# A transformer block on one core: three 1 MB transfers per sequence move from SyncE's queue to ScalarE's

## The chip, the cores and the metric

One core of a Trainium2 chip runs the whole program. The metric is device time in microseconds (us), launch to end.

## The reference, cut to what matters

Sixteen sequences x of 512 tokens by 512 features, float32, go through one attention layer of 32 heads of 16 and one gated feed-forward layer:

```python
q, k, v = split_heads(layernorm(x) @ Wq.T + bq), ...          # 16 sequences, 32 heads of 16
q, k = apply_rope(q, freqs), apply_rope(k, freqs)
weights = softmax(where(causal, q @ k.T / 4, -inf))
x1 = x + layernorm((weights @ v) @ Wo.T + bo)
g, u = layernorm(x1) @ gate_w.T * gate_s, layernorm(x1) @ up_w.T * up_s
out = x1 + layernorm((silu(g) * u) @ down_w.T * down_s)
```

## The kernel before, in words

The program has two phases one after the other: attention (`attention_phase`), which writes x1 to memory, and the feed-forward layer (`ffn_phase`), which reads it. The change touches attention alone.

Each engine runs a list written out by hand. `body(i)`, a pass, has 40 steps: 8 groups of 5 (step s = 5g + u). In each step TensorE makes a piece of the raw scores (`mx`, L864), whose row maxima VectorE takes (L753), and a piece of the transposed scores (`ts`, L878), which ScalarE exponentiates into `probs` (L587, 40 per pass). GpSimd masks `probs` (L465), TensorE weighs the values with them (L892). `ts` has one buffer, so TensorE cannot write the scores of step s+1 before ScalarE has read those of step s. Since there are just 40 exponentials in a pass, their starts mark the steps: below, "group 5 of a pass" is the stretch from its exponential 25 to its exponential 30.

The projections ride in the same steps. Queries and keys are projected for the next pass, get their bias on ScalarE (`biased`, L572), are rotated by GpSimd (`turned`, `roped`, L444 to L453) and VectorE (L735), split into `half` by ScalarE (L581) and VectorE (L740), and go through memory to be laid out anew: SyncE sends `half` to `slots` (L316, L317, at u = 1) and fetches them as `qT` or `kT` (L327, at u = 3), which waits for the sending. The weighed values `oT` (L598) go to memory as `weighed` (L342, at u = 4); their row sums are fetched (`sums`, L349), inverted, sent (`recips`, L355) and fetched again spread over the rows (`spread`, L363) with the values (`averaged`, L364). GpSimd multiplies the two (L484, "the average" below) in groups 1, 3, 5 and 7, at u = 1, ahead of the rotation of its group; ScalarE (L547) and VectorE (L728) split the product.

All transfers stand in SyncE's list (the SP queue), in a fixed order by step. Three of them carry 1 MB, once per pass:

- `xn<-x` at step 9 (L393): the sequence of pass i+2, for its statistics on VectorE at steps 15 and 16 (L705). It waits until `xn` has been transposed (`xT_full`).
- `x<-xr` at step 14 (L396): x1 of sequence i-2 to memory. It waits for GpSimd's residual sums (L491, steps 6 and 11; `x1_ready`).
- `xr<-x` at step 19 (L399): the sequence i-1 for its residual. It waits for the one before (`x1_out`).

There are 15 passes with a `xn` load and 15 with an `xr` load besides the two first loads, which stay where they are (L291, L298), and 16 with an x1 store: 46 transfers. `body` runs from pass -1 to pass 17. A pass before 0 or after 15 has no exponentials.

ScalarE also normalises x (L559, steps 19 to 21) and the projected output (L565, steps 5, 6, 9, 10).

Of the kernel before, what the change touches and what calls it, by code (L numbers as in the profile page):

```python
# [31 lines left out]
NT = T // P  # L32
NC = C // P
# [37 lines left out]
def attention_phase(nc, x, wT, bias_row, bias_columns, rope_cos, rope_sin, slots, weighed, recips, x1):  # L71

    ctx = ExitStack()
    with ctx:
        def sb(name, shape, dt=F32):
            return ctx.enter_context(nc.sbuf_tensor(name, shape, dt))
# [4 lines left out]
        def sem(name):  # L81
            return ctx.enter_context(nc.semaphore(name))
# [21 lines left out]
        xn = sb("xn", [P, NT, C])  # L104
        xr = sb("xr", [P, NT, C])
# [51 lines left out]
        x_in = sem("x_in")  # L157
        xr_in = sem("xr_in")
        x1_out = sem("x1_out")
# [5 lines left out]
        xT_full = sem("xT_full")  # L165
# [42 lines left out]
        x1_ready = sem("x1_ready")  # L208
# [58 lines left out]
        def exists(i):  # L267

            return not isinstance(i, int) or 0 <= i < NB
# [20 lines left out]
        def _(sp):  # L290
# [14 lines left out]
            def send_slots(i, n):  # L305

                ct, which = divmod(n, 2)
                b = n % 2
                halved, fetched = held(sp, 8 * i + n + 1), held(sp, 32 * (NC * i + ct))
                sp.wait_ge(qk_lo, halved)  # L310
                wait_if_any(sp, k_in if which else q_in, fetched)
                rows = slots[which, :, DH:SLOT, :].rearrange("jp (e d s) t -> e jp d (s t)", e=2, s=3)
                both_at, high_at = ((slice(0, 2 * T), slice(2 * T, 3 * T)), (slice(T, 3 * T), slice(0, T)))[which]
                for e in range(2):
                    part = slice(64 * e, 64 * e + 64)
                    sp.dma_start(rows[e][:, :, both_at], half[part, b, :, :]).then_inc(slots_out, 16)  # L316
                    sp.dma_start(rows[e][:, :, high_at], half[part, b, 0, :]).then_inc(slots_out, 16)  # L317
# [12 lines left out]
            def place_shift(i, g):  # L330
                turned_rows, placed = held(sp, NG * i + g + 1), held(sp, 32 * (NG * i + g))
                sp.wait_ge(shift_read, turned_rows)
                wait_if_any(sp, shift_in, placed)
                for pair in range(2):
                    sp.dma_start(qT[SHIFT_ROWS, g // 2, 2 * (g % 2) + pair, :],
                                 shift_rows[4 * pair:4 * pair + 4, g % 2, :]).then_inc(shift_in, 16)

            def send_weighed(i, g):
                ready, fetched = held(sp, NG * i + g + 1), held(sp, 32 * (NC * (i - 1) + g // 2 + 1))
                sp.wait_ge(oT_ready, ready)  # L340
                wait_if_any(sp, averaged_in, fetched)
                sp.dma_start(weighed[g // 2, g % 2, :, :], oT[:, :]).then_inc(weighed_out, 16)  # L342

            def fetch_sums(i, c):
                written = held(sp, 16 * (NC * i + c))
                sp.wait_ge(weighed_out, 16 * (NG * i + 2 * c + 2))
                wait_if_any(sp, recips_out, written)
                heads = weighed[c, :, :, :].rearrange("g (h r) t -> (g h) r t", r=32)
                sp.dma_start(sums[:, :], heads[:, DH, :].rearrange("h (a k) -> h a k", k=8 * T // P)).then_inc(sums_in, 16)  # L349

            def send_recips(i, c):
                divided, fetched = held(sp, NC * i + c + 1), held(sp, 32 * (NC * (i - 1) + c + 1))
                sp.wait_ge(recip_done, divided)
                wait_if_any(sp, averaged_in, fetched)
                sp.dma_start(recips[c], sums[:, :]).then_inc(recips_out, 16)  # L355
# [10 lines left out]
            def body(i):  # L366
                for s in range(NS):
                    g, u = divmod(s, NU)
                    n, owner = QUERIES_KEYS[g - 1]
                    owner += (g - 1) // NG  # L370
                    if u == 4 and exists(i + (g - 1) // NG):
                        send_weighed(i + (g - 1) // NG, (g - 1) % NG)
                    if u == 1 and exists(i + owner):
                        send_slots(i + owner, n)
                    if u == 1 and g in SUMS_AT:
                        c, of = SUMS_AT[g]
                        if exists(i + of):
                            fetch_sums(i + of, c)
                    if u == 1 and g in FETCHED:
                        c, of = FETCHED[g]  # L380
                        if exists(i + of):
                            send_recips(i + of, c)
                    if u == 2 and exists(i + (g + 1) // NG):
                        place_shift(i + (g + 1) // NG, (g + 1) % NG)
                    if u == 3 and exists(i + owner):
                        fetch_slots(i + owner, n)
                    if u == 3 and g in FETCHED:
                        c, of = FETCHED[g]
                        if exists(i + of):
                            fetch_weighed(i + of, c)  # L390
                    if s == 9 and exists(i + 2):
                        sp.wait_ge(xT_full, NC * (i + 2))
                        sp.dma_start(xn[:, :, :], x[i + 2, :, :, :]).then_inc(x_in, 16)  # L393
                    if s == 14 and exists(i - 2):
                        sp.wait_ge(x1_ready, NT * (i - 1))
                        sp.dma_start(x1[i - 2, :, :, :], xr[:, :, :]).then_inc(x1_out, 16)  # L396
                    if s == 19 and exists(i - 2) and exists(i - 1):
                        sp.wait_ge(x1_out, 16 * (i - 1))
                        sp.dma_start(xr[:, :, :], x[i - 1, :, :, :]).then_inc(xr_in, 16)  # L399

            body(-1)
            body(0)
# [135 lines left out]
        def _(act):  # L538
# [23 lines left out]
            def normalise_projected(i, t):  # L562
                if t == 0:
                    act.wait_ge(offset1_ready, i + 1)
                nc.scalar.activation(y[:, t, :], y[:, t, :], ACT.Identity, bias=offset1[:, t:t + 1],  # L565
                                     scale=rstd1[:, t:t + 1]).then_inc(projected_normed, 1)
# [23 lines left out]
            def read_shift(i, g):  # L590
                wait_if_any(act, shift_in, 32 * (NG * i + g - 1))
                act.wait_ge(shift_full, NG * i + g + 1)
                nc.scalar.activation(shift_rows[0:8, g % 2, :], xb16[0:8, bank_of("s", g), 0:T], ACT.Copy).then_inc(shift_read, 1)  # L593
# [6 lines left out]
            def body(i):  # L600
                for s in range(NS):
                    g, u = divmod(s, NU)
                    n, owner = QUERIES_KEYS[g]
                    if u == 2:
                        if exists(i + (g + 1) // NG):
                            read_shift(i + (g + 1) // NG, (g + 1) % NG)
                        if exists(i + owner):
                            add_bias(i + owner, n)
                    if u == 0:
                        kind, ct, of = V_OR_OUT[g - 1]  # L610
                        of += (g - 1) // NG
                        if kind == "v" and exists(i + of):
                            read_v(i + of, ct)
                    if u == 3:
                        if exists(i + (g - 1) // NG):
                            read_weighed(i + (g - 1) // NG, (g - 1) % NG)
                        if TURNED[g]:
                            kind, c, of = TURNED[g]
                            if in_turn(kind, i + of):
                                high_of_x(i + of, c, bank_of(kind, c))  # L620
                    if exists(i):
                        exponential(i, g, u)
                    if u == 4 and exists(i + owner):
                        high_of_roped(i + owner, n)
                    if u == 3 and g in AVERAGED:
                        c, of = AVERAGED[g]
                        if exists(i + of):
                            high_of_attention(i + of, c)
                    if exists(i + 2):
                        for t in NORMALISE_AT.get(s, ()):  # L630
                            normalise_x(i + 2, t)
                    if exists(i - 2):
                        for t in NORMALISE1_AT.get(s, ()):
                            normalise_projected(i - 2, t)

            for t in range(NT):
                normalise_x(0, t)
# [818 lines left out]
```

## Time and profile before

| | |
|---|---|
| runs, median (lowest to highest) | 2681.89 us (2677.47 to 2691.45), 3 runs |
| profiled execution | 2681.5 us, span 2679.8 us |
| attention phase | up to about 1655 us of the span |
| feed-forward phase | from there to the end |
| TensorE busy | 2426.6 us, 91% |
| VectorE, ScalarE, GpSimd busy | 72%, 54%, 43% |

Columns of the views used below: in a table of stretches each engine's busy time stands with its number of instructions, then TensorE's clock as a share of full speed, the busy share of the 16 DMA engines, and GB/s. A wait row names the waiting instruction and the one that ended the wait, then total us, times, longest. A timeline row has start, duration, engine, line, operation, and in brackets the engine's idle time before it with its releaser. SPq is SyncE's queue; the duration of a row there is what issuing the transfer took, not the transfer.

### The profile page before, as it was taken

Reading aid. Unit: us, or ns where it says so; the run is one execution under the profiler, and the core shown is the slowest. Engines: PE = TensorE matmul, PEld = TensorE weight load, DVE = VectorE, ACT = ScalarE, POOL = GpSimd, SP = SyncE. Lnnn points to the kernel's source line nnn. Section 1 sums busy time; section 2 is a strip of 40 time slices with the busy share of each in tenths; the row PEclk is TensorE's granted clock in tenths of the full one; section 3 lists DMA queues with packets and bytes.
Section 4 is the critical chain, followed back from the end, with each engine's and each line's share of the span. In section 5 each row is a group of like instructions: output and inputs, shape, how many; then the busy total and the mean of one; then the engine's idle time right before and its main releaser. Section 6 shows DMA issues by size and latency. Waiting matters only on the chain. (4 is left out here: it accounts for less than half of the span.)

```text
span 2679.8 us, 54601 instructions
## 1 busy us (share of the span) xinstructions
PE 2426.6 (91%) x18816; PEld 1134.6 (42%) x18816; DVE 1931.4 (72%) x5887; ACT 1446.7 (54%) x1902; POOL 1164.6 (43%) x1531
## 2 busy tenths in 40 slices
PE   4889999999999999999999973299999999999997
PEld 2434444444444444444444331144444444444443
DVE  5888889889888888988988853645555555555554
ACT  3577777777777777777777661422222222222221
POOL 3566776777776677677677642000000000000000
PEclk8899999999999999999999987699999999999999
DMA  4444445544554554554454434102111111111111
GB/s 163 120 129 141 159 144 158 168 150 151 167 159 143 166 165 145 159 168 151 143 170 142 142 103 181 72 16 79 47 47 47 63 47 47 73 52 47 47 47 48
DMA packets 178934, 305.62 MB, mean 114 GB/s; under 512 B 32416, under 2 KB 115872, under 8 KB 165536
## 3 DMA queue, kind: packets, MB, share of 16 engines
q1 hardware_dynamic: 178720, 302.86, 34.5%
q8 instruction: 123, 2.02, 0.3%
q14 instruction: 91, 0.75, 0.1%
HBM read 182.73 MB, written 119.01 MB: 113 GB/s over the span
## 5 line engine op out<-in xcount | busy, mean ns | idle before, releaser
L753 DVE CUSTOM_DVE_ANT_0 mx<-mx,causal 128x512 f32<-128x512 f32 (+3 forms) x2048 | 942.6, 517 | 69.7 <-PE mx L864 68.9
L587 ACT ACTIVATE probs<-ts,exp_scale 128x1024 f32<-128x1024 f32 x640 | 710.7, 1111 | 166.8 <-PE ts L878 165.8
L1153 ACT ACTIVATE silu<-gu,gate_scale 128x512 f32<-128x512 f32 x176 | 121.0, 688 | 630.9 <-PE gu L1344 630.9
L1128 POOL TENSOR_TENSOR f_rstd<-f_var,f_neg_half 128x4 f32<-128x4 f32 x32 | 32.3, 1010 | 928.7 <-DVE f_var L1271 646.0
L1294 DVE SCALAR_TENSOR_TENSOR hidden<-gu,up_scale,silu 128x512 f32<-128x512 f32 x176 | 131.9, 749 | 416.6 <-PE gu L1344 406.4
L465 POOL TENSOR_SCALAR_AFFINE_SELECT probs<-probs 128x512 f32<-128x512 f32 x512 | 336.9, 681 | 32.9 <-ACT probs L587 32.7
L892 PE MATMUL xb<-probs,vs 128*32 128x512 f32 (+3 forms) x4096 | 306.4, 440 | 13.4 <-ACT shift_rows L593 12.5
L1342 PE MATMUL gu<-f_xT_hi,gate_hi 128*128 128x512 f16 x704 | 267.7, 380 | 52.5 <-issue 52.5
L878 PE MATMUL ts<-qT,kT 64*128 64x512 f16 (+3 forms) x2048 | 246.0, 298 | 52.9 <-ACT probs L587 50.7
L753 DVE DVE_READ_ACCUMULATOR2_ANT row_max<- 128x1 f32 x2048 | 282.8, 138 | 0.0
L1344 PE MATMUL gu<-f_xT_lo,gate_hi 128*128 128x512 f16 x704 | 267.6, 380 | 0.0
L1356 PE MATMUL down<-down_hi,hid_hi 128*128 128x512 f16 x704 | 266.8, 379 | 0.0
L1342 PE MATMUL gu<-f_xT_hi,up_hi 128*128 128x512 f16 x704 | 266.8, 379 | 0.0
L1344 PE MATMUL gu<-f_xT_lo,up_hi 128*128 128x512 f16 x704 | 266.8, 379 | 0.0
L1360 PE MATMUL down<-down_hi,hid_lo 128*128 128x512 f16 x704 | 266.8, 379 | 0.0
L864 PE MATMUL mx<-kT,qT 64*128 64x512 f16 (+3 forms) x2048 | 252.0, 304 | 8.6 <-DVE row_max L753 7.7
L444 POOL TENSOR_TENSOR turned<-biased,sin_sb 64x512 f32<-64x512 f32 x128 | 163.3, 1276 | 141.8 <-ACT biased L572 135.4
L850 PE MATMUL xb<-xT_hi,w_hi 128*128 128x512 f16 x512 | 199.6, 390 | 11.1 <-issue 9.7
L892 PEld LDWEIGHTS xb<-probs,vs 128*32 128x32 f32 x4096 | 124.8, 110 | 189.8 <-issue 167.7
L850 PE MATMUL xb<-w_hi,xT_hi 128*128 128x128 f16 x1024 | 181.7, 222 | 20.9 <-DVE w_lo L691 11.8
L851 PE MATMUL xb<-xT_lo,w_hi 128*128 128x512 f16 x512 | 197.2, 385 | 0.0
L852 PE MATMUL xb<-xT_hi,w_lo 128*128 128x512 f16 x512 | 196.9, 385 | 0.0
(145 smaller groups left out, 4282.8 us busy)
## 6 DMA issues: line engine op xcount, KB each, us to landing
slots<-half SPq DMA_DIRECT2D x260, 128.0 KB, 13.7
qT<-slots SPq DMA_DIRECT2D x128, 256.0 KB, 3.6
kT<-slots SPq DMA_DIRECT2D x128, 256.0 KB, 3.7
weighed<-oT SPq DMA_DIRECT2D x128, 256.0 KB, 4.5
xn<-x SPq DMA_DIRECT2D x16, 1024.0 KB, 7.4
xr<-x SPq DMA_DIRECT2D x16, 1024.0 KB, 7.8
slots<-half SPq DMA_DIRECT2D x256, 64.0 KB
spread<-recips SPq DMA_DIRECT2D x64, 256.0 KB
```

The costliest lines, as they stand in the source:

```text
L465: nc.gpsimd.affine_select(out=d, in_=d, compare_op=ALU.is_ge, fill=0.0, base=0, pattern=[[0, HG], [1, P]], channel_multiplier=-1).then_inc ...
L587: nc.scalar.activation(probs[:, g % 2, u, :, :], ts[:, :, :], ACT.Exp, scale=exp_scale[:, 0:1]).then_inc(ts_read, 1)
L753: last = nc.vector.tensor_tensor_reduce(out=scores, in0=scores, in1=causal[:, T - P * (qt + 1):T], scale=1.0, scalar=-3e38, op0=ALU.add, o ...
L850: nc.tensor.matmul(out, a_hi, b_hi, start=first, stop=False)
L851: nc.tensor.matmul(out, a_hi, b_lo, start=False, stop=False)
L864: last = nc.tensor.matmul(mx[:, 2 * (n % 2) + j, at:at + P * (qt + 1)], qT[rows, ct, p, P * qt:P * (qt + 1)], kT[rows, ct, p, 0:P * (qt + ...
L878: last = nc.tensor.matmul(ts[:, j, at:at + T - P * kt], kT[rows, ct, p, P * kt:P * (kt + 1)], qT[rows, ct, p, P * kt:T], start=True, stop= ...
L892: last = nc.tensor.matmul(bank[32 * h:32 * h + 32, P * kt:T], vs[:, g // 2, kt, HG * (g % 2) + h, :], probs[:, g % 2, u, j, at:at + T - P ...
L1342: nc.tensor.matmul(gu[:, bank, :], hi[:, c, cols], xT_hi[:, c, :], start=c == 0, stop=False)
L1344: last = nc.tensor.matmul(gu[:, bank, :], hi[:, c, cols], xT_lo[:, c, :], start=False, stop=end and not with_rest)
L1356: nc.tensor.matmul(down[:, t, :], hid_hi[:, b % 3, rows], down_hi[:, b, :], start=b == 0, stop=False)
L1360: last = nc.tensor.matmul(down[:, t, :], hid_lo[:, b % 3, rows], down_hi[:, b, :], start=False, stop=b == NI - 1)
```

## The change

The three transfers leave SyncE's list and stand at the end of a step in ScalarE's, with the same waits. The first keeps its step, 9. The store of x1 moves from step 14 to 15, the load of `xr` from step 19 to 24. At the end of a step means behind the exponential of that step, and behind whatever else ScalarE does in it.

```diff
@@ SyncE, body(i) @@
-                    if s == 9 and exists(i + 2):
-                        sp.wait_ge(xT_full, NC * (i + 2))
-                        sp.dma_start(xn[:, :, :], x[i + 2, :, :, :]).then_inc(x_in, 16)
-                    if s == 14 and exists(i - 2):
-                        sp.wait_ge(x1_ready, NT * (i - 1))
-                        sp.dma_start(x1[i - 2, :, :, :], xr[:, :, :]).then_inc(x1_out, 16)
-                    if s == 19 and exists(i - 2) and exists(i - 1):
-                        sp.wait_ge(x1_out, 16 * (i - 1))
-                        sp.dma_start(xr[:, :, :], x[i - 1, :, :, :]).then_inc(xr_in, 16)
@@ ScalarE, body(i) @@
+                    if s == 9 and exists(i + 2):
+                        act.wait_ge(xT_full, NC * (i + 2))
+                        act.dma_start(xn[:, :, :], x[i + 2, :, :, :]).then_inc(x_in, 16)
+                    if s == 15 and exists(i - 2):
+                        act.wait_ge(x1_ready, NT * (i - 1))
+                        act.dma_start(x1[i - 2, :, :, :], xr[:, :, :]).then_inc(x1_out, 16)
+                    if s == 24 and exists(i - 2) and exists(i - 1):
+                        act.wait_ge(x1_out, 16 * (i - 1))
+                        act.dma_start(xr[:, :, :], x[i - 1, :, :, :]).then_inc(xr_in, 16)
```

SyncE, before, steps 13 to 16 of a pass (ISA and REGISTER_ALU rows are waits and counting):

```order
L327 DMA kT<-slots 64x4x512 x2
L359 REGISTER_ALU
L363 DMA spread<-recips 128x1x512
L364 DMA averaged<-weighed 128x1x512
L342 DMA weighed<-oT 128x512
L396 ISA
L396 DMA x<-xr 128x2048
L48 ISA
L316 DMA slots<-half 8x8x1024
L317 DMA slots<-half 8x8x512
```

With the change:

```order
L327 DMA kT<-slots 64x4x512 x2
L359 REGISTER_ALU
L363 DMA spread<-recips 128x1x512
L364 DMA averaged<-weighed 128x1x512
L342 DMA weighed<-oT 128x512
L48 ISA
L316 DMA slots<-half 8x8x1024
L317 DMA slots<-half 8x8x512
```

The store is gone from between the fetch for the average and the sending of `half`; the order of the rest is as it was.

ScalarE with the change, steps 9 and 10 (L628 is the moved load; L556, L543 and L578 are L565, L552 and L587 of before):

```order
L556 ACTIVATE projected<-projected,offset,rstd 128x512
L628 DMA xn<-x 128x2048
L543 ACTIVATE vs<-xb 128x32x16
L578 ACTIVATE probs<-ts,exp_scale 128x1024
L556 ACTIVATE projected<-projected,offset,rstd 128x512
```

The load stands between two activations ahead of exponential 10. Steps 24 and 25:

```order
L578 ACTIVATE probs<-ts,exp_scale 128x1024 x2
L572 ACTIVATE half<-roped 128x512
L634 DMA xr<-x 128x2048
L578 ACTIVATE probs<-ts,exp_scale 128x1024 x2
L584 ACTIVATE shift_rows<-xb 8x512
```

The load of `xr` is now issued between the last activation of group 4 and exponential 25.

## Rows read from the trace of the kernel before

**Rows 1.** Busy time of each engine in one stretch of 96 us, a pass long

```profile
680.00:776.00 96.00, 91.53 (x904) 42.95 (x902) 85.18 (x309) 72.82 (x93) 70.39 (x93) 1.00 0.50 159
```

**Rows 2.** Waits of TensorE between 296 and 1448 us, twelve passes

```profile
PE ts L878 <- ACT probs L587: 25.5, 27, 2.9
PE xb L892 <- ACT shift_rows L593: 10.5, 14, 0.9
```

**Rows 3.** Waits of GpSimd in the same stretch

```profile
POOL averaged L484 <- DMA averaged<-weighed: 123.9, 44, 6.3
```

**Rows 4.** Waits of SyncE's queue in the same stretch, for the sending of `half`

```profile
SPq L327 <- DMA slots<-half: 55.1, 35, 3.5
```

**Rows 5.** DMA issues of the page: queue, times, KB each, median us to landing

```profile
xn<-x SPq DMA_DIRECT2D x16, 1024.0 KB, 7.4
xr<-x SPq DMA_DIRECT2D x16, 1024.0 KB, 7.8
...
x<-xr SPq DMA_DIRECT2D x16, 1024.0 KB, 8.4
...
out<-f_xr SPq DMA_DIRECT2D x16, 1024.0 KB, 3.9
...
recips<-sums SPq DMA_DIRECT2D x64, 16.0 KB, 2.1
```

**Rows 6.** Timeline, group 5 of pass 2 and of pass 14: exponentials 25 and 30, the average

```profile
336.90 1.11 ACT L587 ACTIVATE probs<-ts,exp_scale 128x1024 f32<-128x1024 f32 x1 [0.37 <-PE ts L878]
340.67 1.28 POOL L484 TENSOR_TENSOR averaged<-averaged,spread 128x512 f32<-128x512 f32 x1 [2.65 <-DMA averaged<-weighed]
347.81 1.11 ACT L587 ACTIVATE probs<-ts,exp_scale 128x1024 f32<-128x1024 f32 x1 [0.37 <-PE ts L878]
...
1484.35 1.11 ACT L587 ACTIVATE probs<-ts,exp_scale 128x1024 f32<-128x1024 f32 x1 [1.61 <-PE ts L878]
1491.83 1.27 POOL L484 TENSOR_TENSOR averaged<-averaged,spread 128x512 f32<-128x512 f32 x1 [7.76 <-DMA averaged<-weighed]
1498.08 1.10 ACT L587 ACTIVATE probs<-ts,exp_scale 128x1024 f32<-128x1024 f32 x1
```

**Rows 7.** Timeline, group 3 of pass 9, then of pass 11 with two transfers ahead of it

```profile
982.52 1.11 ACT L587 ACTIVATE probs<-ts,exp_scale 128x1024 f32<-128x1024 f32 x1
986.51 1.29 POOL L484 TENSOR_TENSOR averaged<-averaged,spread 128x512 f32<-128x512 f32 x1 [3.05 <-DMA averaged<-weighed]
994.88 1.11 ACT L587 ACTIVATE probs<-ts,exp_scale 128x1024 f32<-128x1024 f32 x1
...
1170.42 0.61 SPq L364 DMA_DIRECT2D averaged<-weighed  x1
1171.73 0.35 SPq L396 DMA_DIRECT2D x<-xr  x1
1172.84 1.11 ACT L587 ACTIVATE probs<-ts,exp_scale 128x1024 f32<-128x1024 f32 x1
1177.85 1.28 POOL L484 TENSOR_TENSOR averaged<-averaged,spread 128x512 f32<-128x512 f32 x1 [4.08 <-DMA averaged<-weighed]
1186.14 1.10 ACT L587 ACTIVATE probs<-ts,exp_scale 128x1024 f32<-128x1024 f32 x1
```

**Rows 8.** Timeline at step 9 of pass 7: ScalarE's second-last activation, TensorE's scores

```profile
777.84 0.80 ACT L565 ACTIVATE projected<-projected,offset,rstd 128x512 f32<-128x512 f32 x1
...
780.18 0.39 PE L878 MATMUL ts<-qT,kT 64*128 64x512 f16 x2 [1.40 <-ACT probs L587]
```

**Rows 9.** Timeline of the start: SyncE's load, ScalarE's weights, VectorE's statistics of sequence 1

```profile
18.03 0.35 SPq L393 DMA_DIRECT2D xn<-x  x1
23.08 7.68 ACT L642 ACTIVATE w_hi<-probs,scale 128x2048 f16<-128x2048 f32 x4 [4.45 <-DVE scale L67]
40.90 2.46 DVE L705 BATCH_NORM_STATS2 stats<-xn 128x6 f32<-128x512 f32 x4
```

**Rows 10.** Timeline near the end of attention: the last average

```profile
1627.19 1.26 POOL L484 TENSOR_TENSOR averaged<-averaged,spread 128x512 f32<-128x512 f32 x1 [4.00 <-DMA averaged<-weighed]
```

## The prediction

> **What bounds the kernel now.** I read the table of stretches first, to see how much of a pass is waiting at all. In 96 us TensorE is busy for 91.5 at full clock, so at most 4.5 us of a pass can be won, and no other engine is full: VectorE has 85, ScalarE 73, GpSimd 70 [rows 1]. The DMA engines are half busy. Attention is bound by TensorE, with short stalls.
>
> Then TensorE's own waits, over twelve passes. None names a transfer. The largest is the scores waiting for an exponential, 25.5 us in all, 2.1 a pass [rows 2]. So a gain or a loss can only come through the engines that feed TensorE, ScalarE first, and the question is which of those waits for a transfer. It is GpSimd: the average waits 123.9 us for its two fetches in 44 of its turns [rows 3]. And SyncE's queue waits 55.1 us, in 35 of 96 turns, for the sending of `half` to land before it may fetch it back; the fetch for the average stands behind that in the list [rows 4]. A 1 MB transfer in the same queue takes 7.4 to 8.4 us from issue to landing, against 3.9 for one of the same size that has the DMA engines to itself (the last phase's store) and 2.1 for 16 KB [rows 5]. From the last two, the data of 1 MB occupy the engines for about 3.9 - 2.1 = 1.8 us; that is my estimate of what one such transfer puts ahead of another, and with the 8.4 of the store in attention the most would be 8.4 - 2.1 = 6.3.
>
> **How a late average costs time.** This is the reading on which the numbers rest. I measured groups by their exponentials. Group 5 of pass 2 takes 347.81 - 336.90 = 10.9 us, and its average starts 3.8 us into it. Group 5 of pass 14 takes 13.7 us, and its average starts at 7.5 [rows 6]. The average 3.7 us later makes the group 2.8 us longer: all but about 0.9 us of the delay arrives at the next exponential, since GpSimd's rotation, ScalarE's `half` and the exponential stand behind it. Those are the first and last of the 13 passes 2 to 14 in which this group has its full work; read in the same way, ten of the 13 lie within half a microsecond of 10.9, one is at 12.3, two at 13.7 and 13.8, and the excess over 10.9 sums to some 9 us, 0.7 a pass. Group 3 has no slack left: average 4.0 us into the group, length 12.4 (pass 9); average 5.0 us in, length 13.3 (pass 11) [rows 7]. One microsecond later, one longer.
>
> **The change part by part.**
>
> *Taken from SyncE.* 46 issues of 0.35 us, as the store's row has it [rows 7], 16 us of SyncE's time. It gates nothing: after issuing, this queue mostly waits for `half`. Worth 0. In passes 2 to 14 the load of `xr` no longer stands between the sums and the sending of `half` in group 4, so the fetch of `kT` and behind it the fetch for the average of group 5 can go earlier. If that brings every group 5 to 10.9, the gain is 9 us.
>
> *The Trainium skill* says that transfers issued from different engines run on the same 16 DMA engines and interleave, so that spreading them saves issue time alone ("DMA: Bandwidth & Descriptors", section "Issuing engines are not separate DMA queues"). By that, this gain would be 0. No row of the trace can show it, as all data here go through one queue.
>
> *Put on ScalarE.* The same 46 issues, between activations of 0.8 us or behind an exponential of 1.11. No row shows ScalarE issuing a transfer. Below: 0, since the issue of 0.35 us is shorter than the activation running then, and ScalarE's queue can pass it while that runs. Above: it is added where ScalarE is late already. That is step 9: behind its `projected` activation TensorE's next scores wait 1.4 us for ScalarE [rows 8]; 14 passes times 0.35 is 5 us. All 46 at full price would be 16. I take 0, nearest to the row that shows 0.8 us of cover. The waits in front of the three are met: `xn` is transposed at step 7, the residual sums end at step 11, and the store of step 15 has nine steps, over 20 us, before step 24 asks for it, and took 8.4. Behind each wait would stand the exponentials, so a miss here would be dear, but I see none.
>
> *The store, step 14 to 15.* Before, it is issued 1.3 us behind the fetch for the average of group 3, in the same queue and so after it [rows 7]. Now it is issued with the first exponential of group 3, 1.1 us later, but in another queue, where nothing keeps it behind. Below: the average comes 0.3 us earlier, down to the 12.4 of pass 9: 14 x 0.3 = 4 us won. Above: the store's data go in front of it, 1.8 us in each of 14 passes: 25 us lost. I take 0, near the lower end, because by the time the store's data start, some 1 us after issue (half of the 2.1 of 16 KB), the fetch has been under way for 3.5.
>
> *The load of `xr`, step 19 to 24.* It leaves group 4 (the 9 us above) and is now issued right ahead of exponential 25, at the very time at which the fetch for the average of group 5 has just been issued at step 23. Below 0. Above, 1.8 us later: of that the slack of 0.9 is taken off, 0.9 x 13 = 12 us lost. Between them I take the whole 12 against the gain of 9, because this load, unlike the store, comes when the fetch has just started: +3.
>
> *The load of `xn`, step 9.* Later than before, because ScalarE's issue stands behind its own work of step 9. Its data are wanted at step 15, five steps of 96 / 40 = 2.4 us on, and took 7.4 of these 12. 0. But it now runs beside the sending of `half` in group 2: up to 0.5 us, unpriced, in the range.
>
> *Start and end.* The load for sequence 1 waited for nothing at 18 us; on ScalarE it stands behind the four weight activations, which end at 30.8. Landing 7.4 us later, at 38, it is still ahead of the statistics at 40.9 [rows 9]. 0. At the end the last average waits 4.0 us for its fetch and everything stands behind it [rows 10]; the store beside it costs 0 to 1.8 us. I take 0.
>
> Sum: 0 + 0 + 0 + 3 = +3 on the profiled execution's 2681.5, which lies 0.4 us below the median of the runs: **2685 us**.
>
> **The rivals.** A measurement of this kernel can tell about 0.5% from no change, 13.4 us, so the borders are 2668.5 and 2695.3.
>
> 1. *Forecast: the two queues cost about what they save.* 2675 to 2695. For it: no wait of TensorE names a transfer, and the moves are small beside 96 us. Chance 0.45.
> 2. *Slower: the average loses its place.* In one queue the fetch for the average always came before the store. In two, 1 MB gets in front of it in groups 3 and 5. From the point where the average starts beyond 4.0 us into group 3 or beyond 4.7 into group 5, each microsecond counts: 14 x 1.8 + 12 - 9 = +28, 2710 us; at the larger price it is worse. For it: group 3 has no slack. Against it: the store comes 3 us behind the fetch. Chance 0.2.
> 3. *Slower by turns.* The transfers of both queues take turns on a DMA engine, a whole share at a time. Then the store, which arrives when `averaged` is being moved, comes after it and costs nothing, while the load of `xr`, which arrives during `spread`, gets between `spread` and `averaged`: 0 + 12, with the gain of 9 or without: 2685 to 2694, and more where 1 MB takes over 1.8 us. The Trainium skill states such turns: each DMA engine goes round its queue rows packet by packet (same page, section "Queues, rings and completion order"). No row can show it here. Chance 0.12.
> 4. *Faster: the long transfers out of the way.* The gain of 9, with nothing lost in group 5, 4 in group 3, and averages of the other groups a little earlier as well: 2681.5 - 15 = 2666 us. For it: 35 waits of SyncE for its sending, and the two long groups 5. Chance 0.18.
> 5. *ScalarE pays for the issues.* Either it cannot go on during an issue, 5 to 16 us, or a wait is not met. 2687 to 2698. Chance 0.05.
>
> **How the numbers follow.** Faster by over 0.5%: case 4 with its middle just beyond the border, 0.18. Slower by over 0.5%: case 2 whole, a third of case 3, half of case 5 and the upper edge of case 1: 0.32. The same: 0.50. The range takes case 4 and most of case 2: 2666 to 2714.
>
> **What would show it.** Right: ScalarE's list passes the three issues with its next exponential no later; TensorE's wait at step 10 still about 1.4 us; the waits of SyncE for the sending of `half` well under 55 us; group 5 at 11 to 12 us in every pass, without the two of 13.7 and 13.8; group 3 as before, the average 4.0 to 5.0 us in. Wrong: average 3 starting 6 us into its group (case 2); group 5 near 10.9 throughout and the average at 3.8 or before (case 4); TensorE's wait for the exponential at step 10 up by 0.35 us or more (case 5); or a new wait of ScalarE for `x1_ready` or `x1_out`.

## The result, and the profile after

| | before | changed |
|---|---|---|
| median of 18 runs, us | 2687.34 | 2697.22 |
| lowest and highest | 2677.47 to 2693.21 | 2691.04 to 2708.76 |
| profiled execution: span, us | 2679.8 | 2691.0 |
| attention ends, us into the span | 1655.78 | 1667.22 |

The changed kernel takes 1.0044 times as long, with a 95% interval of 1.0032 to 1.0056: 11.8 us longer, small but resolved. It is inside the range, 12 us above the forecast of 2685; about 5 us of the 12 are the kernel before itself, whose median in these runs is 2687.3 and not the 2681.9 of the three runs that the forecast started from. In the profiled executions attention becomes 11.4 us longer and the whole span 11.2, so the phase behind it is as it was, and everything below is about attention.

A pass seen in stretches, for the kernel after (columns as in [rows 1]); TensorE is a little less busy in 96 us, nothing else stands out:

```profile
584.00:680.00 96.00, 89.97 (x877) 41.56 (x875) 85.15 (x303) 71.29 (x91) 68.88 (x92) 1.00 0.49 152
680.00:776.00 96.00, 91.24 (x900) 42.72 (x898) 85.23 (x309) 72.48 (x93) 70.73 (x93) 1.00 0.51 157
```

The waits of TensorE and GpSimd after, from 296 to 1448 us as in [rows 2, 3] (us in total, times, longest):

```profile
POOL averaged L475 <- DMA averaged<-weighed: 134.1, 45, 5.9
...
PE ts L878 <- ACT probs L578: 33.6, 36, 1.8
```

And those of SyncE's queue, which answer to [rows 4]:

```profile
SPq L316 <- DVE half L740: 347.9, 95, 6.4
SPq L327 <- DMA slots<-half: 30.1, 21, 3.3
SPq L349 <- DMA weighed<-oT: 27.7, 26, 2.7
```

SyncE waits 25 us less for the sending of `half`, which the prediction counted on, and yet the average waits 10 us more than the 123.9 of [rows 3], and TensorE 8 us more for an exponential. What SyncE saved was not what the average was waiting for.

Section 3 of the page, the queues: packets, MB, and the time of the packets as a share of the 16 DMA engines' span. The 46 transfers have a row of their own now:

```profile
q1 hardware_dynamic: 172096, 254.62, 30.0%
q10 hardware_dynamic: 6624, 48.24, 4.8%
```

4.8% of 2691 us is 129 us, for 46 transfers 2.8 us each. This is the time that the packets of a 1 MB transfer take on a DMA engine in the mean, where the prediction took 1.8. From issue to landing, in the page's DMA issues (queue, times, KB each, median us), it takes less than in SyncE's queue for `xn` and the store, and no less for `xr`:

```profile
x<-xr ACTq DMA_DIRECT2D x16, 1024.0 KB, 7.3
...
xn<-x ACTq DMA_DIRECT2D x15, 1024.0 KB, 4.8
xr<-x ACTq DMA_DIRECT2D x15, 1024.0 KB, 8.0
```

**Where the 11 us lie.** I measured all groups by the starts of their exponentials, as in the prediction. Mean lengths over passes 2 to 13, in us; groups 0 to 4 differ by 0.02 at most:

| group | 5 | 6 | 7 | sum of all 8, twelve passes |
|---|---|---|---|---|
| before | 11.40 | 11.66 | 10.98 | 1152.4 |
| after | 12.25 | 11.85 | 10.92 | 1164.5 |

Group 5 carries 10.2 of the 12.1 us, group 6 another 2.3. The timeline of group 5 of pass 5 after, SyncE's queue first, then ScalarE with its queue, then GpSimd (start, length, engine, line, operation, [idle before it]):

```profile
620.22 0.62 SPq L363 DMA_DIRECT2D spread<-recips  x1
620.88 0.61 SPq L364 DMA_DIRECT2D averaged<-weighed  x1
...
621.88 1.12 ACT L578 ACTIVATE probs<-ts,exp_scale 128x1024 f32<-128x1024 f32 x1 [0.83 <-PE ts L878]
621.97 0.33 ACTq L634 DMA_DIRECT2D xr<-x  x1
623.87 1.11 ACT L578 ACTIVATE probs<-ts,exp_scale 128x1024 f32<-128x1024 f32 x1 [0.37 <-PE ts L878]
...
636.32 1.10 ACT L578 ACTIVATE probs<-ts,exp_scale 128x1024 f32<-128x1024 f32 x1
...
630.06 1.26 POOL L475 TENSOR_TENSOR averaged<-averaged,spread 128x512 f32<-128x512 f32 x1 [5.06 <-DMA averaged<-weighed]
```

The fetch is now early: `spread` is issued 3.7 us before exponential 25 (623.87). But the average starts 9.8 us behind it, against 6.3 to 6.8 in eleven of twelve passes before, so 6.2 us into the group, 1.5 beyond the slack of 4.7; the group takes 12.5 us, 1.6 above 10.9. The load of `xr` is issued 1.8 us behind `spread` and 1.1 behind `averaged`, and yet the average waits as if the load, or much of it, had gone first.

**Two measures are used below.** *Lag*: from the issue of `spread` to the issue of the 1 MB transfer next to it. *Delay*: from the issue of `spread` to the start of the average. Over passes 2 to 13 the mean delay in group 5 is 6.6 us before and 9.3 after; in group 3, where the store is the neighbour, 7.4 before and 7.2 after.

### The profile page after: what moved, and what is told of

The parts are those of the page before. It is cut to its first block and busy times, and to the rows that moved or that the text cites. A ratio compares the mean times of both kernels' runs of the same rounds, so it can differ in the third digit from the quotient of the medians.

```text
span 2691.0 us, 54505 instructions
## 1 busy us (share of the span) xinstructions
PE 2431.1 (90%) x18816; PEld 1134.4 (42%) x18816; DVE 1937.2 (72%) x5887; ACT 1445.9 (54%) x1902; POOL 1166.1 (43%) x1531
## 5 line engine op out<-in xcount | busy, mean ns | idle before, releaser
L578 ACT ACTIVATE probs<-ts,exp_scale 128x1024 f32<-128x1024 f32 x640 | 710.7, 1110 | 163.1 <-PE ts L878 162.5
L850 PE MATMUL xb<-xT_hi,w_hi 128*128 128x512 f16 x512 | 199.5, 390 | 11.6 <-issue 9.9
L850 PE MATMUL xb<-w_hi,xT_hi 128*128 128x128 f16 x1024 | 181.7, 222 | 20.2 <-DVE w_lo L691 11.8
```

Of the source, the lines that this page charges most:

```text
L578: nc.scalar.activation(probs[:, g % 2, u, :, :], ts[:, :, :], ACT.Exp, scale=exp_scale[:, 0:1]).then_inc(ts_read, 1)
L850: nc.tensor.matmul(out, a_hi, b_hi, start=first, stop=False)
```

## The experiments

The theory, *turns*, is rival 3 of the prediction: the queues take turns, and the load of `xr`, issued while `spread` is being moved, gets in before `averaged` or a part of it. Its rivals: *the moment*, 1 MB beside the fetch, in whatever queue; and *the issues*, which cost ScalarE time. Ratios are to the kernel before, run beside each.

### The load of `xr` at the same step, in SyncE's queue

```
-  ScalarE: if s == 24 ...: act.wait_ge(x1_out, ...); act.dma_start(xr, x[i - 1])
+  SyncE:   if s == 24 ...: sp.wait_ge(x1_out, ...);  sp.dma_start(xr, x[i - 1])
```

> The changed kernel, with the load of xr issued at the same step 24, but by SyncE, in the queue of the fetch for the average and behind it. Theory A (turns): the load costs 0.8 us per group 5 because it is in another queue and gets between the fetches of spread and averaged. Then here it stays behind both: spread issue to average back from 9.4 to 10.3 us to 6.4 to 7.5, group 5 at 10.9 to 11.1, time 2678 to 2686, 0.4% to 0.7% faster than the changed kernel. Theory B (the moment): two transfers under way at once slow each other, whichever queue they come from. Then the average stays 9 to 10 us behind the issue of spread, group 5 at 12 to 12.5, and the time within 3 us of the changed kernel. Theory C (ScalarE pays for issuing): gain of the load's issue alone, 14 x 0.35 = 5 us at most, group 5 unchanged.

Measured: 2678.81 us against 2682.03, ratio 0.9989 [0.9975, 1.0003]. The same pass, the same group:

```profile
620.78 0.63 SPq L363 DMA_DIRECT2D spread<-recips  x1
621.45 0.61 SPq L364 DMA_DIRECT2D averaged<-weighed  x1
622.83 0.34 SPq L393 DMA_DIRECT2D xr<-x  x1
...
624.43 1.11 ACT L581 ACTIVATE probs<-ts,exp_scale 128x1024 f32<-128x1024 f32 x1 [0.37 <-PE ts L878]
...
635.35 1.11 ACT L581 ACTIVATE probs<-ts,exp_scale 128x1024 f32<-128x1024 f32 x1 [0.37 <-PE ts L878]
...
627.86 1.29 POOL L478 TENSOR_TENSOR averaged<-averaged,spread 128x512 f32<-128x512 f32 x1 [2.30 <-DMA averaged<-weighed]
```

Issued with a lag of 2.0 to 2.1 us in every pass, behind `averaged` in one queue, the load leaves the delay at 7.1 us here (mean 7.2), and group 5 takes 10.9 us in each of the twelve passes. The time is 0.55% under the changed kernel's, as the theory of turns foretold. The lag is 0.2 to 0.3 us more than in most passes of the changed kernel, and no run has the load at a lag of 2.05 us in ScalarE's queue. The nearest, one pass each of the kernels with the store at step 14 and with `xr` back in SyncE (both below), have 1 MB of ScalarE at a lag of 2.3 and 2.2 us and delays of 7.1 and 7.0. So this run by itself does not tell the queue from the 0.3 us; what happens in the passes that are hit is read from the packets further below.

### The load one and three steps later, in ScalarE's queue

```
-  if s == 24 and exists(i - 2) and exists(i - 1):
+  if s == 25 and exists(i - 2) and exists(i - 1):      (second kernel: s == 27)
```

> The changed kernel, with the load of xr one step later on ScalarE, behind exponential 25. It then arrives about 2 us later, when averaged is being moved. Theory A (turns, a transfer's share on a DMA engine at a time): it waits for the share of averaged that is being moved and costs nothing: average 6.4 to 7.5 us behind the issue of spread, group 5 at 10.9 to 11.3, time 0.4% to 0.7% under the changed kernel. Theory A2 (turns row by row): the rows of both alternate from its arrival on, so the part of averaged that is left takes longer: average 8 to 9 us behind, group 5 at 11.3 to 12. Theory B (the moment): as A2 or worse. Theory C: no change against the changed kernel.

> The changed kernel, with the load of xr behind exponential 27 on ScalarE, when the fetch for the average of group 5 has landed. Theories A, A2 and B agree: nothing of the load meets the fetch: average 6.4 to 6.8 us behind the issue of spread, group 5 at 10.9, 1.3 us less than the changed kernel in each of 13 passes, 17 us, and some 0.4 us less than the kernel before, 5 to 8 us: 2679 to 2684. Theory C (ScalarE pays for issues): as the changed kernel, 2695 to 2699.

Measured: 1.0007 [0.9996, 1.0018] and 1.0008 [0.9991, 1.0026]. Step 25, the same group:

```profile
618.06 0.62 SPq L363 DMA_DIRECT2D spread<-recips  x1
...
621.71 1.11 ACT L578 ACTIVATE probs<-ts,exp_scale 128x1024 f32<-128x1024 f32 x1 [0.37 <-PE ts L878]
621.73 0.33 ACTq L634 DMA_DIRECT2D xr<-x  x1
...
632.62 1.11 ACT L578 ACTIVATE probs<-ts,exp_scale 128x1024 f32<-128x1024 f32 x1 [0.36 <-PE ts L878]
...
625.43 1.29 POOL L475 TENSOR_TENSOR averaged<-averaged,spread 128x512 f32<-128x512 f32 x1 [2.61 <-DMA averaged<-weighed]
```

With a lag of 3.1 to 5.5 us the mean delay is 6.8, and group 5 takes 10.9 us in all 13 passes. Step 27, lag 7.2 to 8.8, gives 6.6 and 11.2. All three issues are still ScalarE's, so the issues are not the cause; in the second queue the load costs what it costs by being 2 us too early. Both kernels gain a little less against the changed one than was expected: 0.37% where it was 0.4% to 0.7%, and 0.36%, 10 us, where it was 17. With the load at step 25 SyncE waits for the sending of `half` almost as long as before (55.1 in [rows 4]):

```profile
SPq L327 <- DMA slots<-half: 52.4, 37, 3.9
```

so that sum says nothing about the length of group 5, for which the prediction had read it.

### The store, drawn into the same place in group 3

```
-  if s == 15 and exists(i - 2):
+  if s == 14 and exists(i - 2):
```

> The changed kernel, with the store of x1 one step earlier on ScalarE (14, its step on SyncE before), all else as changed. It then arrives before or while spread of group 3 is being moved. Theory A (turns): it gets ahead of averaged as the load of xr does in group 5: average of group 3 from 7.4 to about 9.5 to 10 us behind the issue of spread, group 3 from 12.7 to about 15, 2.3 us in 14 passes, +30 us, 2722 to 2732. Theory B (the moment): in the kernel before the store was issued at this very step from SyncE and group 3 took 12.7; then about 12.7 to 13 here too, within 5 us of the changed kernel. Theory C: no change.

Measured: 2706.87 us, ratio 1.0099 [1.0072, 1.0126]. Group 3 of pass 5:

```profile
599.47 0.63 SPq L363 DMA_DIRECT2D spread<-recips  x1
600.14 0.60 SPq L364 DMA_DIRECT2D averaged<-weighed  x1
...
600.49 0.35 ACTq L631 DMA_DIRECT2D x<-xr  x1
602.44 1.11 ACT L578 ACTIVATE probs<-ts,exp_scale 128x1024 f32<-128x1024 f32 x1
...
617.76 1.10 ACT L578 ACTIVATE probs<-ts,exp_scale 128x1024 f32<-128x1024 f32 x1
...
609.61 1.27 POOL L475 TENSOR_TENSOR averaged<-averaged,spread 128x512 f32<-128x512 f32 x1 [6.24 <-DMA averaged<-weighed]
```

The lag is 1.0 us, the delay 10.1 (mean 9.2, against 7.2 with the store at step 15), and the group takes 15.3 us: the damage can be made in group 3 at will, as turns would have it. The price was half of what was expected (1.0099 against the changed kernel's 1.0044, so 15 us for 30). Groups 3 and 4 lost 2.55 us a pass, but in every pass group 5 came back to 10.9: a longer group 3 had shifted the load's lag in group 5 to 2.3 to 4.6 us, and it no longer met the fetch. A loss at one place took away a loss at the other.

### Only parts of the change

```
first kernel:   the load of xr back in SyncE at step 19; xn (9) and the store (15) on ScalarE
second kernel:  the kernel before, with the load of xr alone on ScalarE, at step 24
```

> The load of xr back on SyncE at step 19 as in the kernel before; the load of xn (step 9) and the store of x1 (step 15) stay on ScalarE. If the loss of the change is the load of xr alone, this is the kernel before again: group 5 at 11.2 to 11.6 on average with a few of 12 to 14, group 3 at 12.5 to 12.9, ratio to before 0.998 to 1.002. If the two others cost or gain anything on ScalarE, it shows as the rest of the 0.44%: a ratio of 1.002 to 1.004 if they cost.

> The kernel before, with only the load of xr moved to ScalarE at step 24. If the loss is this load alone, getting between spread and averaged: the average of group 5 9.4 to 10.3 us behind the issue of spread, group 5 at 12 to 12.5, ratio to before 1.003 to 1.006, as the whole change. If the loss needs all three on ScalarE: 1.000 to 1.002.

Measured: 1.0007 [0.9989, 1.0024] without the move of `xr`, 1.0043 [1.0024, 1.0062] with it alone. This one transfer is the whole loss. With it alone, lag and delay in group 5, pass by pass (from the timeline, us):

| pass | 2 | 3 | 4 | 5 | 6 | 7 | 8 | 9 | 10 | 11 | 12 | 13 |
|---|---|---|---|---|---|---|---|---|---|---|---|---|
| lag | 2.7 | 1.8 | 0.3 | 1.8 | 2.7 | 1.7 | 1.8 | 1.7 | 1.8 | 1.7 | 1.3 | 0.2 |
| delay | 7.1 | 7.3 | 10.5 | 9.6 | 7.1 | 7.1 | 7.3 | 8.5 | 7.6 | 9.8 | 10.8 | 10.7 |
| group 5 | 10.9 | 10.9 | 14.5 | 12.2 | 10.9 | 10.9 | 10.9 | 11.4 | 10.9 | 12.4 | 13.8 | 16.3 |

At a lag of 2.7 the load is harmless, at 1.3 and less it always costs 3.5 us or so, and at 1.7 to 1.8 the delay is anything from 7.1 to 9.8; the mean, 8.6, is below the 9.4 to 10.3 that was expected. In the changed kernel ten of twelve passes have a lag of 1.3 to 1.8 and a delay of 9.4 to 10.3; pass 2, at 2.8, has 6.7; pass 9, at 1.8, has 6.9. In the kernel with `xr` back in SyncE the store met the fetch once, at a lag of 1.7: delay 9.5, and that group 3 took 16.0 us.

**What the packets show.** The trace also has every packet that the DMA engines moved, with its queue, and the profile counts them in any stretch. For pass 5 of the changed kernel, from 624.55 to 626.65 us and from there to 628.55 (q1 is SyncE's queue, q10 ScalarE's; packets, MB, share of the 16 engines):

```profile
q10 hardware_dynamic: 60, 0.49, 68.9%
q1 hardware_dynamic: 133, 0.25, 33.5%
...
q10 hardware_dynamic: 72, 0.52, 67.0%
q1 hardware_dynamic: 8, 0.01, 2.3%
```

The load is 128 packets of 8 KB, eight for each of the 16 engines, 0.31 us each where nothing disturbs them; the fetch is packets of 2 KB, 0.08 us each. No packet names its engine, but where one ends another begins, within 0.01 us, and so they can be chained. From 625.43 to 629.24 us there is one strict alternation, a packet of the load, a packet of the fetch, eight of each; the eight of the load take 3.1 us. Meanwhile the fetch had ended elsewhere: of the last eight counts of its semaphore, each for a part that has landed, seven come by 6.4 us behind the issue of `spread`, the eighth at 9.8, and the average starts.

The other passes agree. In the ten passes of the changed kernel that were hit, one to five of the last eight counts are late (8.8 to 10.3 us; the rest 5.2 to 7.3), and the longest alternation that can be chained has 12 to 27 packets. It has 5 and 7 in its passes 2 and 9, 3 to 5 in its group 3, 3 to 6 in group 5 with the load in SyncE's queue at step 24, and 17 to 29 in group 3 with the store at step 14. With the load at step 25 in ScalarE's queue it is 1 to 5: there the load meets the fetch on no engine for long, and so theory A2, right about single packets, foretold too much for that step. The fit is not perfect. With the load of `xr` alone on ScalarE the five passes with delays of 9.6 and more have 13 to 24, but pass 10, at 7.6, has 14, and pass 9, at 8.5, has 8.

Yet with the load in SyncE's queue at step 24, 52 to 91 of its 128 packets begin before the fetch has landed, in every pass. Where both were in SyncE's queue, the two did not alternate like this: 3 to 7 packets at most, over the twelve passes each of group 3 in the kernel before and of that group 5. So 1 MB beside the fetch costs little; what costs is that on some DMA engines the packets of the two queues take turns while the fetch is unfinished there, and the slowest engine decides. The turns are of single packets: rival 3's "a whole share at a time" is not what happens. This would also explain why the outcome at one lag differs from pass to pass: it would depend on whether some engine still has the fetch to do when the load reaches it.

### The load in four quarters

```
-  act.dma_start(xr[:, :, :], x[i - 1, :, :, :]).then_inc(xr_in, 16)
+  for t in range(NT): act.dma_start(xr[:, t, :], x[i - 1, :, t, :]).then_inc(xr_in, 16)
GpSimd:  - pool.wait_ge(xr_in, 16 * (i + 1))    + pool.wait_ge(xr_in, 16 + 16 * NT * i)
```

> The changed kernel, with the load of xr at step 24 on ScalarE as four loads of 256 KB in a row. Theory A (turns, a transfer's share at a time): only a quarter gets between spread and averaged, the next comes behind averaged: a quarter of the 3.3 us, average 6.8 to 7.7 us behind the issue of spread, group 5 at 11 to 11.5, ratio to before 0.998 to 1.002, so 0.3% to 0.5% under the changed kernel. Theory B (the moment, both share the DMA engines by bytes): the same 1 MB at the same moment, average 9 to 10 us behind, group 5 at 12.2, ratio 1.004. The three more issues on ScalarE, 1 us a pass ahead of an activation, cost up to 0.6 us a pass if they are not covered.

Measured: 1.002 [1.0001, 1.0039], mean delay 8.1 (6.4 to 10.0 by pass), group 5 at 11.5. Two of the twelve lags are 0.1 and 0.2 us, with delays of 10.0 and 9.7, two more 0.9 and 1.2, but at 1.7 to 1.8, where seven of eight of the changed kernel's were 9.4 or more, the seven of this kernel are 6.4 to 8.4. The ratio is at the upper edge of what turns foretold, and the delay above the 6.8 to 7.7. The edit does more than it says: it also makes the load's packets four times smaller. The load is now 512 packets of 2 KB, 0.08 us each at the shortest. If sixteen packets of the fetch take turns with sixteen of these, 16 x 0.08 = 1.3 us go in front, where eight of 8 KB were 8 x 0.31 = 2.5; this is an estimate from the packets' lengths, and the mean delay rose over the 6.6 of before by 1.5 here and by 2.7 in the changed kernel. So the run is consistent with turns of single packets, and does not show that four pieces as such help. Group 4 takes 12.56 us in the mean, against 12.30 in the changed kernel, and in pass 5 exponential 25 starts 2.14 us behind 24 (621.82), against 2.00. That the four issues cause this is not shown: the row below puts the wait down to TensorE's scores.

```profile
621.91 1.46 ACTq L635 DMA_DIRECT2D xr<-x  x3
623.40 0.45 ACTq L635 DMA_DIRECT2D xr<-x  x1
623.96 1.11 ACT L578 ACTIVATE probs<-ts,exp_scale 128x1024 f32<-128x1024 f32 x1 [0.51 <-PE ts L879]
```

### Both transfers at later steps

The first kernel is the changed one with the store at step 17 and the load at 25, both on ScalarE. The second is the kernel before, all in SyncE's queue:

```
-  if s == 14 and exists(i - 2):                        +  if s == 17 and exists(i - 2):
-  if s == 19 and exists(i - 2) and exists(i - 1):      +  if s == 25 and exists(i - 2) and exists(i - 1):
```

> The changed kernel, with the load of xr at step 25 and the store of x1 at step 17, both on ScalarE behind the fetches for the averages. Group 5 at 10.9 as with the load at 25 alone. If the store beside the fetch costs group 3 anything (average 6.5 us behind the issue of spread without it, 7.3 with it): group 3 from 12.7 to 12.2 to 12.4, 0.3 to 0.5 us in 14 passes, 4 to 7 us less, ratio to before 0.996 to 0.999. If group 3 has another limit at 12.3 or the gain is taken back later: 0.999 to 1.001, and group 3 unchanged.

> The kernel before, all three transfers in SyncE's list, with only the steps moved: the store of x1 from 14 to 17 and the load of xr from 19 to 25, so both are issued when the fetch for the average of their group is about to land. If what the best version gains (ratio 0.9963) is the moment alone, this gives the same: average of group 3 about 6.5 us behind the issue of spread, group 3 at 12.2, group 5 at 10.9, ratio 0.995 to 0.998. If ScalarE's queue is needed for it, because in SyncE's the fetches of steps 18 and 28 and the sending of half at step 26 stand behind a long transfer: waits of SyncE for the sending at 55 us or more as before, the average of group 5 later again, ratio 0.998 to 1.001.

Measured: 2674.24 us against 2683.67, ratio 0.9963 [0.9944, 0.9982], and 2673.17 against 2686.66, ratio 0.9942 [0.9922, 0.9962]. Both are faster than the kernel before run beside them, by 0.4% and 0.6%, and so faster than the changed one. The second, group 3 of pass 5:

```profile
591.01 0.63 SPq L363 DMA_DIRECT2D spread<-recips  x1
...
600.93 0.36 SPq L396 DMA_DIRECT2D x<-xr  x1
...
594.37 1.11 ACT L587 ACTIVATE probs<-ts,exp_scale 128x1024 f32<-128x1024 f32 x1 [0.20 <-issue]
...
606.00 1.11 ACT L587 ACTIVATE probs<-ts,exp_scale 128x1024 f32<-128x1024 f32 x1
...
597.49 1.28 POOL L484 TENSOR_TENSOR averaged<-averaged,spread 128x512 f32<-128x512 f32 x1 [2.47 <-DMA averaged<-weighed]
```

and its waits in the stretch of [rows 3, 4]:

```profile
POOL averaged L484 <- DMA averaged<-weighed: 113.6, 45, 4.2
...
SPq L327 <- DMA slots<-half: 32.0, 30, 3.5
```

The store now comes 9.9 us behind `spread`, 3.4 us after the average has begun, and this group takes 11.6 us; the mean delay in group 3 is 6.7 and group 3 takes 12.4 us, against 12.7 before, group 5 11.05 against 11.40. ScalarE's queue is not needed for any of this.

The load is another matter. SyncE's list runs ahead of the exponentials, so at step 25 it is issued 2.0 us behind `spread` in every one of the twelve passes, right behind the fetch in the same queue, and not when the fetch is about to land, as was expected. It has left group 4, and it keeps its place behind the fetch (mean delay 7.1). In the first kernel it is 2.7 to 3.8 us behind, in the other queue (6.8). Nor does the second kernel's profile account for its gain. Its passes 2 to 13 sum to 1150.6 us, against 1152.4 before and 1143.6 in the first kernel: groups 3 and 5 give 7.5 us, and groups 0 to 2 take as much back. The profiled execution, 2677.74 us, is the slowest of its six.

## Why the prediction was right or wrong

The forecast was +3 us on balance; the case that held was the third rival, slower by turns, at its upper end and a little beyond (2685 to 2694, "and more where 1 MB takes over 1.8 us"). Its chance was put at 0.12. That the measured time is inside the range owes something to luck in the sum: the forecast itself, two queues that cost about what they save, did not hold, and the loss and the relief were both there and did not balance.

*Taken from SyncE, gain up to 9.* Half right. SyncE's 16 us of issues gated nothing. The 13 groups 5 of passes 2 to 14 sum to 150.5 us before and to 141.9 in the kernel with the load at step 25, so a relief of 8.6 is there in its profiled execution, the fastest of that kernel's ten. But it comes with the load's absence from group 4, and not from the 55.1 us of waits that I read as its measure.

*Put on ScalarE, 0.* Right. The issue runs beside an activation and ScalarE does not pause for it; at step 9 of pass 5 after, the load of `xn` is issued during `half`, 0.5 us before the `projected` activation that stands ahead of it in the list has begun, and the scores wait 1.5 us there, as in [rows 8]:

```profile
586.19 0.63 ACT L572 ACTIVATE half<-roped 128x512 f16<-128x512 f32 x1 [1.26 <-POOL roped L444]
586.25 0.34 ACTq L628 DMA_DIRECT2D xn<-x  x1
586.73 0.80 ACT L556 ACTIVATE projected<-projected,offset,rstd 128x512 f32<-128x512 f32 x1
```

Over passes 2 to 13, TensorE's idle time at step 10 sums to 17.5 us before and 17.4 after. No wait for `x1_ready` or `x1_out` appeared.

*The store, 0.* Right: it comes 2.7 to 3.1 us behind `spread` in eleven of twelve passes, and there is no long alternation of packets in group 3. The reason given, that the fetch has then long been under way, fits, but the fetch is not over: the store's first packet moves 3.6 to 4.0 us behind `spread`, and the average starts at 7.2 in the mean, where it can be 6.6. The margin was thinner than I knew; with the store one step earlier, at a lag of 1.0, it cost 2 us of delay.

*The load of `xr`, +12 against 9.* This step failed, by size. The direction and the place were right. The 13 groups 5 sum to 160.4 us after, 18.5 above the 141.9 of the undisturbed ones: the loss was 18.5 instead of 12, the relief 8.6 instead of 9, and the net +9.9 instead of +3. Group 6 adds 2.3 that the forecast did not have. The mis-sized term is the 1.8 us for what 1 MB puts ahead: I had it from the difference of two landing times, 3.9 - 2.1 [rows 5]. The queue's own row gives 2.8 us, eight packets of 0.31 us are 2.5 at the least and took 3.1 in pass 5, and the delay grew by 2.7 in the mean and by 3.2 in the ten passes that were hit. The packets of the kernel before say the same, 0.31 us at the shortest and 0.345 in the mean, so the term could have been had beforehand. The rule for what a late average costs held: in pass 5, 1.5 us beyond the slack made the group 1.6 longer.

*The load of `xn`, start and end, 0.* Right within what can be seen. At the start the load was issued at once, ahead of three of the four weight activations that I thought it would stand behind:

```profile
23.07 2.00 ACT L642 ACTIVATE w_hi<-probs,scale 128x2048 f16<-128x2048 f32 x1 [4.63 <-DVE scale L67]
23.08 0.39 ACTq L628 DMA_DIRECT2D xn<-x  x1
```

and the statistics of sequence 1 start at 40.26 instead of 40.90 [rows 9]. The last average of attention waits 4.13 us for its fetch, beside 4.00 [rows 10].

*The Trainium skill.* The rule by which the gain of SyncE's queue would be 0 is that of "DMA: Bandwidth & Descriptors", section "Issuing engines are not separate DMA queues". It is right that the same engines serve both queues: packets of both alternate there. The relief of 8.6 us in the groups 5 speaks against a gain of 0, the median of the kernel that has it (1.0007) for it; and the order of service does change with the queue. The other rule of that page (section "Queues, rings and completion order"), that an engine goes round its queue rows packet by packet, agrees with the trace, in which 8 packets of the load and 8 of the fetch alternate one by one. What rests on an inference is which packets belong to one DMA engine: they were matched by the end of one and the start of the next.

**Left open.** With the load at step 25, group 5 is at 10.9 us throughout and the profiled execution of that kernel is 10 us shorter than that of before, but its median in ten runs is not (2682.63 against 2682.03). That profile is the fastest of its ten executions, runs of the kernel before spread over 16 us, and what takes the gain back in the other executions was not found. The reverse holds for the last kernel, both transfers later in SyncE's queue: 13 us faster in the median, 2 us in passes 2 to 13 of its profile. What decides at a lag of 1.7 to 1.8 whether an engine is late with the fetch was not found either. And no run has the load in SyncE's queue at that lag: the issues of the two fetches and of `weighed` stand ahead of it and take it to 2.0.

## What to carry to other kernels

Moving a long transfer to another engine's queue frees issue time, but it also gives up the transfer's place behind what was issued before it: in this case packets of the two queues took turns, and the fetch waited for the DMA engine that was last. Before doing so, list the short fetches that someone waits for and their issue times: here 1 MB behind such a fetch by 1.8 us or less delayed its use by about 3 us in ten of eleven passes of the changed kernel; behind it by 2.7 us, or in the fetch's own queue by 2.0, it cost 0.8 us or less in the mean. If the long transfer has time to spare, change its step first and leave its queue: the store three steps and the load six steps later gave 0.6%, and the queue of ScalarE added nothing to it.

## What the runs showed of the hardware that was not expected

- An issue on ScalarE takes 0.33 to 0.39 us of its queue, runs beside an activation, and may go out before the activation that precedes it in the program has begun or ended (586.25 against 586.73 us). Four in a row took 1.9 us in pass 5, and the group with them was 0.26 us longer in the mean.
- The order within one queue is not free either: before, the store stood behind the fetch of group 3 in SyncE's queue, at a lag of 2.0 us, and the delay was 7.4 us in the mean; with the store 7 us or 10 us behind it was 6.6 and 6.7. So 0.7 to 0.8 us were being paid there, and the length of 12.4 us that the prediction took as the floor of group 3 was none: it came down to 11.6 in the best pass.
- Two queues took turns on a DMA engine by single packets: one of 8 KB (0.31 us) for one of 2 KB (0.08 us). A fetch in small packets beside a load in large ones then waits mostly for the load (an estimated 2.5 us for eight such packets).
- Losses of this kind can cancel: the kernel with the store at step 14 lengthened groups 3 and 4 by 2.55 us and brought group 5 back to 10.9, since the load's lag grew with the time that the groups before had lost.
